# A sorted edge list visited in pairs of tiles: PE sums each pair in one PSUM bank, VectorE adds once a pair

## What is computed

```python
q = (h @ Wq + bq).reshape(N, H, C)
k = (h @ Wk + bk).reshape(N, H, C)
v = (h @ Wv + bv).reshape(N, H, C)
score = jnp.einsum('ehc,ehc->eh', q[dst], k[src]) / np.sqrt(C)
m = jax.ops.segment_max(score, dst, num_segments=N)
ex = jnp.exp(score - m[dst])
denom = jax.ops.segment_sum(ex, dst, num_segments=N)
msg = (ex / denom[dst])[:, :, None] * v[src]
agg = jax.ops.segment_sum(msg, dst, num_segments=N)
```

## Time and profile before

| | |
|---|---|
| median of 3 runs | 8399.73 us |
| profiled execution, its own time | 8395.49 us |
| its span | 8393.8 us |
| edge stage, first gather to last add | 650.2 to about 1988 us |
| busy share of the span | PE 70%, VectorE 63%, GpSimd 62%, ScalarE 37% |

### The profile page before, as it was taken

The page is one execution under the profiler, slowest core; times in us unless marked ns, Lnnn a source line. Parts: engine busy times, 40 slices in busy tenths (PEclk is TensorE's granted clock), DMA queues, the critical chain, the costliest instruction groups (busy, mean ns, idle before and its releaser), DMA issues. The chain is left out here.

```text
span 8393.8 us, 114926 instructions
## 1 busy us (share of the span) xinstructions
PE 5911.5 (70%) x29083; PEld 4485.9 (53%) x29083; DVE 5252.3 (63%) x14320; ACT 3102.5 (37%) x9138; POOL 5186.5 (62%) x5153
## 2 busy tenths in 40 slices
PE   6586777774399555556688888965577775574398
PEld 5234555553387234444577777754455553453387
DVE  9867888887665576665544444446677777435544
ACT  1245888887422300000333333312344444312322
POOL 0475666665577677777677777756777771433422
PEclk9798999996599877778699999967789986686599
DMA  5475666563366333333111111116333343473366
GB/s 147 152 247 160 171 173 172 170 172 115 108 207 200 111 102 101 100 102 103 28 28 32 31 28 32 26 27 193 102 105 103 105 100 117 150 229 95 100 204 199
DMA packets 633946, 1017.21 MB, mean 121 GB/s; under 512 B 136434, under 2 KB 436482, under 8 KB 631948
## 3 DMA queue, kind: packets, MB, share of 16 engines
q0 software_dynamic: 241920, 540.19, 24.2%
q1 hardware_dynamic: 391436, 470.18, 17.7%
HBM read 790.98 MB, written 222.86 MB: 121 GB/s over the span
## 5 line engine op out<-in xcount | busy, mean ns | idle before, releaser
L4099 POOL DMA_INDIRECT gat_edges_rows<-gat_table,gat_room x1080 | 1115.5, 1033 | 340.9 <-issue 322.4
L2825 POOL DMA_INDIRECT l_edges_ring<-pairs,first_room x832 | 843.8, 1014 | 472.5 <-issue 242.2
L2387 POOL DMA_INDIRECT l_sum_rows<-l_feats,back_room x832 | 827.0, 994 | 265.7 <-issue 241.9
L2407 PE MATMUL l_sum_o<-l_sum_rows,l_sum_s 128*128 128x256 f32 x1664 | 604.4, 523 | 468.3 <-DVE l_sum_s L2418 220.4
L2876 ACT ACTIVATE l_edges_ring<-l_edges_ring,l_edges_weight 128x64 f32<-128x64 f32 x3328 | 816.4, 335 | 0.0
L2407 PEld LDWEIGHTS l_sum_o<-l_sum_rows,l_sum_s 128*128 128x128 f32 x1664 | 410.9, 261 | 655.0 <-DVE l_sum_s L2418 325.5
L2948 PE MATMUL l_edges_o<-l_edges_ring,l_edges_sf 128*128 128x260 f32 x1664 | 534.9, 427 | 149.8 <-DVE l_acc L3081 141.1
L3717 ACT ACTIVATE m_ffn_ht<-m_ffn_hp,m_ffn_b1t 128x256 f32<-128x256 f32 (+1 forms) x598 | 270.7, 453 | 815.5 <-PE m_ffn_hp L3684 810.3
L2429 DVE TENSOR_TENSOR l_acc<-l_acc,l_sum_o 128x256 f32 x832 | 350.1, 421 | 351.3 <-PE l_sum_o L2407 258.4
L3694 PE MATMUL m_ffn_yp<-m_ffn_w2b,m_ffn_ht 128*128 128x256 f32 x2156 | 502.1, 385 | 30.4 <-ACT m_ffn_ht L3717 29.8
L3684 PE MATMUL m_ffn_hp<-m_ffn_xt,m_ffn_w1b 128*128 128x256 f32 (+1 forms) x2392 | 509.0, 366 | 11.5 <-DVE m_ffn_xt L3733 7.2
(11 more groups left out here) (899 smaller groups left out, 14604.4 us busy)
## 6 DMA issues: line engine op xcount, KB each, us to landing
sorted_rows<-l_proj_zero SPq DMA_DIRECT2D x44, 1032.0 KB
m_ffn_w1b<-in_L_ffn_w SPq DMA_DIRECT2D x32, 1024.0 KB, 6.4
m_ffn_w2b<-in_L_ffn_w SPq DMA_DIRECT2D x32, 1024.0 KB, 5.4
m_ffn_xs<-sorted_rows SPq DMA_DIRECT2D x120, 258.0 KB, 3.6
m_ffn_w1b<-in_L_ffn_W SPq DMA_DIRECT2D x57, 512.0 KB, 4.6
m_ffn_w2b<-in_L_ffn_W SPq DMA_DIRECT2D x57, 512.0 KB
m_by_node<-gat_edges_ys SPq DMA_DIRECT2D x96, 256.0 KB
l_proj_taken<-m_by_node SPq DMA_DIRECT2D x28, 768.0 KB, 6.9
```

The costliest lines, as they stand in the source:

```text
L2387: pool.indirect_dma_start(rows[:, slot, j, :], None, table, bass.IndirectOffsetOnAxis(ap=L.src[:, t:t + 1], axis=0)).then_inc(got[slot], 16)
L2407: pe.matmul(o[:, j, 0:D], s4[:, q % S4, j, :], rows[:, slot, j, :], start=True, stop=True).then_inc(out_done, 1)
L2825: pool.indirect_dma_start(rows(q, 0, 2 * D)[:, j, :], None, table, bass.IndirectOffsetOnAxis(ap=L.src[:, t:t + 1], axis=0)).then_inc(got[q ...
L4099: pool.indirect_dma_start(rows[:, slot, j, :], None, table, bass.IndirectOffsetOnAxis(ap=L.src[:, q * B + j:q * B + j + 1], axis=0)).then_ ...
```

## The change

The list `first` is made with `group=2`. Every block now begins at a pair of tiles, so both tiles of a pair belong to one block. The list has (391 pairs + 49) x 2 = 880 tiles, 220 quads, 55 chunks. PE sums the two tiles of a pair into one bank (`start` on the first, `stop` on the second), and VectorE adds once for a pair. The other lists keep `group=1`. To make room, `U` goes from 14 to 13.

```diff
-        self.tiles = -(-(self.cols + T) // (2 * Q)) * 2 * Q
+        self.tiles = -(-(-(-self.cols // group) + T) * group // (2 * Q)) * 2 * Q
...
-        did(dve.tensor_reduce(self.ended[:], self.cmp, AX.X, ALU.add))
+        did(dve.tensor_reduce(self.ended[:], self.cmp[:, :, L.group - 1::L.group], AX.X, ALU.add))
...
-            did(dve.tensor_tensor(self.tile, const.slot[:, at], n, ALU.subtract))
+            did(dve.scalar_tensor_tensor(out=self.tile, in0=n, scalar=-float(L.group), in1=const.slot[:, at],
+                                         op0=ALU.mult, op1=ALU.add))
...
-    H, W, n, CQ, U, BK = 4, D, L.quads, 4, 14, 2
+    H, W, n, CQ, U, BK, G = 4, D, L.quads, 4, 13, 2, L.group
...
                     for j in range(Q):
-                        t = q * Q + j
-                        if t >= BK:
-                            pe.wait_ge(acc_own, t - BK + 1)
-                        pe.matmul(o[:, t % BK, 0:W + H], sf[:, q % 2, j, :], rows(q, 0, W + H)[:, j, :], start=True, stop=True
-                                  ).then_inc(out_done, 1)
+                        k, i = divmod(q * Q + j, G)
+                        if i == 0 and k >= BK:
+                            pe.wait_ge(acc_own, k - BK + 1)
+                        pe.matmul(o[:, k % BK, 0:W + H], sf[:, q % 2, j, :], rows(q, 0, W + H)[:, j, :], start=(i == 0),
+                                  stop=(i == G - 1)).then_inc(out_done, 1)
                         if j:
                             yield
...
-                    for j in range(Q):
-                        t = q * Q + j
-                        dve.wait_ge(out_done, t + 1)
-                        if t:
-                            dve.wait_ge(acc_own, t)
+                    for j in range(0, Q, G):
+                        k = (q * Q + j) // G
+                        dve.wait_ge(out_done, (k + 1) * G)
+                        if k:
+                            dve.wait_ge(acc_own, k)
                         a = acc[:, ds(b[j], 1), :]
-                        dve.tensor_tensor(a, a, o[:, t % BK, 0:W + H].unsqueeze(1), ALU.add).then_inc(acc_own, 1)
+                        dve.tensor_tensor(a, a, o[:, k % BK, 0:W + H].unsqueeze(1), ALU.add).then_inc(acc_own, 1)
                         yield
...
-        first, back = SortedList(nc, "first", E), SortedList(nc, "back", E)
+        first, back = SortedList(nc, "first", E, group=2), SortedList(nc, "back", E)
```

More of the change, by code:

```diff
@@ L662, with __init__ @@
 class SortedList:
-    def __init__(self, nc, name, edges):
-        self.name, self.edges = name, edges
+    def __init__(self, nc, name, edges, group=1):
+        self.name, self.edges, self.group = name, edges, group
         self.cols = -(-edges // P)
-        self.tiles = -(-(self.cols + T) // (2 * Q)) * 2 * Q
+        self.tiles = -(-(-(-self.cols // group) + T) * group // (2 * Q)) * 2 * Q
         self.quads = self.tiles // Q
@@ L694, with __init__ @@
 class SortConstants:
-    def __init__(self, nc, ctx, core, tiles, when):
+    def __init__(self, nc, ctx, core, tiles, when, group=1):
         sb = lambda n, s, dt=F32: ctx.enter_context(nc.sbuf_tensor(f"sort_{n}_{when}", s, dt))
@@ L720, in _ @@
                     dve.tensor_copy(self.slot[:], slot_i[:])
-                    dve.tensor_scalar(self.tile_of[:], tile_i[:], -1.0, None, ALU.add)
+                    dve.tensor_scalar(self.tile_of[:], tile_i[:], -float(group), None, ALU.add)
                     for k in range(8):
@@ L909, in vector @@
         dve.wait_ge(self.summed, 1)
-        did(dve.tensor_tensor(self.first[:], self.banks[0:T, 0, 0:1], core.part[0:T, :], ALU.add))
+        did(dve.tensor_scalar(self.first[:], self.banks[0:T, 0, 0:1], core.part[0:T, :], float(L.group), ALU.add, ALU.mult))
         settled()
@@ L2766, in edge_attend @@
     AWAY = (LANE_SLOTS - 1) * LANE_SETS
-    assert n % CQ == 0
+    assert n % CQ == 0 and Q % G == 0 and L.tiles // 2 <= 512
     with Phase(nc, name) as ph:
@@ L3066, in add @@
                         if q:
-                            dve.wait_ge(acc_own, q * Q)
+                            dve.wait_ge(acc_own, q * Q // G)
                         a = acc[:, ds(b[0], 1), :]
@@ L3185, in layer0_gnn @@
     with ExitStack() as cs:
-        const = SortConstants(nc, cs, core, first.tiles, "a")
+        const = SortConstants(nc, cs, core, first.tiles, "a", first.group)
         project(nc, core, "l0_proj", core.x, 4 * D,
```

## The result

| | before | after |
|---|---|---|
| median | 8402.59 us (4 runs) | 8532.39 us (4 runs) |
| range | 8396.39 to 8413.97 us | 8516.60 to 8546.80 us |
| profiled execution, span | 8393.8 us | 8514.9 us |

The ratio is 1.0155, with a 95% interval of 1.0141 to 1.0168: slower by 130 us, where 102 were forecast. The profiled executions differ by 8514.9 - 8393.8 = 121.1 us.

The account below looks back on a forecast made before the run. ScalarE was taken to bound a calm chunk (22.59 us). With later scans 24.24, plus 0.54 and 0.29, C is 25.07; 54 chunks take 1353.8 us, 102.5 more than before, hence 8502 us; range 8405 to 8570.

Parts of the forecast that it names:

- Three more chunks: Steady stretch: 54 chunks between first and last `spread` instead of 51, a loss of 73.6 us at the old chunk length.
- Fewer adds: VectorE: four adds a quad become two, 3.3 us less work a chunk; PE's `collect` stops waiting for its own step's adds.
- The scans behind the late wait: VectorE: scans behind the last add delay `reach_back` by 0.79 and `lower` by 0.86 us, making a calm chunk 24.24 us.
- What an average chunk still loses: Added to the calm chunk: 0.54 us for PE's low clock behind `reach_back`, 0.29 for GpSimd's stalls; C is 25.07 us.
- PE's pauses for adds go: Argument about PE against a low clock in every chunk: its waits for adds, 137.2 us before, would disappear.
- the clock rival: Slower still: longer PE pauses bring the low clock in every chunk, C 26.36 us, 172 us more, 8572 us; chance 0.15.
- The faster one: Rival: the scans' delay falls where ScalarE is busy anyway, C 22.59 us, 31 us less, 8368 us; chance 0.12.
- The middle one: No-change rival: only `reach_back` moves and nearly all losses go, C 23.1 to 23.5 us, 8396 to 8417 us; chance 0.13.
- The 48 gathers at nothing: GpSimd: 48 more gathers cost nothing, since 16 need about 21.7 us, hidden under a chunk; uncovered 65 us.
- the break-even of the prediction: Steady stretch: the chunk length at which 54 chunks take the old 1251.3 us, C = 23.17 us.

Follow-up runs that it names:

- e3: The kernel before with only the longer list of 880 tiles, each tile added by itself in the old order; ratio to before 1.0097.
- e1: The changed kernel with the scans of `across` and `under` written ahead of the quad's last add on VectorE; ratio to before 1.0009.
- e5: The changed kernel with the scans ahead of the last add only in the step of `across`; ratio to before 1.0057.
- e2: The kernel before, 832 tiles and an add a tile, with both scans put behind the quad's last add; ratio to before 1.0064.
- e7: The changed kernel with ten small matmuls once a chunk in PE's pause ahead of a turn; ratio to before 1.0124.
- a1: The unaltered change measured once more beside the other kernels on one chip; 8517.75 us, ratio to before 1.0115.
- e9: The changed kernel with scans ahead of the last add, ten filling matmuls on PE and ScalarE's `widen` first; ratio to before 1.0015.
- e8: The changed kernel with scans ahead of the last add and ten filling matmuls in PE's pause; ratio to before 1.0011.
- e4: The changed kernel with scans ahead of the last add and ScalarE's `widen` ahead of `spread` and `expo`; ratio to before 0.9991.
- e12: e9's kernel with 12 gathers a chunk instead of 16, part of the input left out; one run, 8353.67 us.

## Why the prediction was right

**Three more chunks: right.** 54 chunks for 51, and the list by itself cost 76.0 us (e3) where 3 x 24.53 = 73.6 were reckoned.

**Fewer adds: right.** PE's wait for adds went from 137.2 us to nothing. Pairs together with the better order of e1 are worth 54.9 us (e1 against e3); the pairs by themselves were not measured.

**The scans behind the late wait: right, and the term that decides.** Reckoned were 2.51 and 2.37 us from the last `collect` to `reach_back` and `lower`; measured 2.53 and 2.44. The calm chunk was forecast at 24.24 us and is 24.23 or 24.24. That the two delays add was an argument from the order; e5 and e1 show it, and e2 shows that pairs are not needed for it.

**What an average chunk still loses: mis-sized.** The step that failed is "15 x 1.83 / 51 = 0.54 us a chunk. I keep it." The mean loss over the calm chunk is 25.51 - 24.235 = 1.28 us, forecast 0.83. Five copies that waited 2.3 to 2.5 us near a stall of GpSimd cost about 2.4 us each, 0.22 us a chunk (0.29 was forecast). The first chunk of the stage took 0.48 us extra, 0.01 a chunk. The remaining 1.05 us are PE's low clock, twice the forecast. Where the forecast had put it, behind `reach_back`, it came 12 times at 2.91 - 1.08 = 1.83 us, 0.41 us a chunk. What it had at nothing is the low clock behind the turn of the `meet` step: 20 copies that waited 1.40 us, 0.52 us a chunk. (The other 0.1 us are small growths of other waits.) The count of 15 came from a kernel in which PE was held by adds now and then. Without that hold PE comes to the turn of the `meet` step early and stands still for 2.04 us until ScalarE has copied, in the change, in e1 and in e5 alike; in the chunk of the earlier trace rows that wait was 1.09 us, and in most chunks of e2, with an add a tile, 0.7 to 1.1. So "PE's pauses for adds go", which the prediction held against the clock rival, spoke for it: the idle time did not vanish, it gathered in one place. The prediction looked for new pauses only ahead of `reach_back` and `lower`. e7 shows that the low clock behind this one costs 29 to 36 us by itself. The sum 54 x (25.51 - 25.07) = 23.8 us is nearly the whole gap of 126.4 - 102.5 = 23.9 us in the stretch.

**The rivals.** The faster one had its condition, `reach_back` at most 0.3 us later behind its turn; it came 0.8 us later. The slower one, a low clock behind `reach_back` in every chunk, came in 12 of 54: its mechanism was there, but mostly at another pause. The middle one had only `reach_back` move; both moved, and C came out at 25.5 and not at 23.1 to 23.5. That the whole time came out 28 us above the forecast says little by itself, because the same change measured 96 us in a1, below the 102 forecast; the chunk is what was tested.

**The 48 gathers at nothing: right here, and only here.** Under a chunk of 25.5 us they are hidden: VectorE waited 61.3 us for rows in the change and 65.1 before. In e9 they and what hangs on them are the bound, and probably in e8 and e4, at 23.16 us a chunk rather than the 21.7 us that 16 x 1.35 gave, since gathers also wait for scores and for room in the ring.

## What to carry to other kernels

Where programs are written out in turns, taking pieces out of one function moves its last wait ahead of its neighbours' pieces; look at what was interleaved with the pieces that go, and put a chain that hands over to another engine ahead of a wait that it does not need. Price a change at the calm period first, then ask of each engine that gets idle time where its longest pause will stand, because the clock may fall there. And before trading work of one engine for more tiles, ask what period the next bound would leave: here, with the gathers, it was 23.16 us, and the break-even of the prediction was 23.17.

## What the runs showed of the hardware that was not expected

- A pause of PE of 2.04 us ahead of a turn stood in nearly every chunk of the change, but the lower granted clock followed it in 25 of 53 chunks only; in e1, with the same pause, in 43 of 53. Pauses of 1.65 us at another turn of the chunk (752.54 in the change) left the granted clock at 1.00 each time, and in the kernel before a pause of only 0.58 us ahead of `reach_back` (1322.25) was followed by 0.50. Ten matmuls of 0.72 us in the pause of 2.04 us took the waits of 1.40 us from 20 to none. Why one such pause is followed by the lower clock and the next is not stays open.
- GpSimd's issue stalls of 2.2 to 3.6 us came seven times in the stretch of every other kernel here, and not once in e12, whose longest is 1.4 us by its list of waits, 720 to 1940 us:

```profile
POOL l_edges_ring L2826 <- issue: 138.0, 435, 1.4
```

There GpSimd issues a quarter less and often waits for room in the ring. What the stalls are stays open.
